# Edge network with one target product per block, numbers to compare in PSUM, and a reordered ScalarE round in attention 1

## The reference

```python
# edge network
edge_in = concatenate([h[src], h[dst], edge_features])
h1 = relu(edge_in @ We1 + be1)            # 32 wide
edge_msg = relu(h1 @ We2 + be2)           # 128 wide
h2 = relu(concatenate([h[dst], edge_msg]) @ Wn1 + bn1)   # 64 wide
out = h + segment_sum(relu(h2 @ Wn2 + bn2), dst)
# attention 1 (4 heads, ELU, softmax with the segment's maximum)
e = elu(s_src[src] + s_tgt[dst]);  ex = exp(e - segment_max(e)[dst])
out = segment_sum(ex / segment_sum(ex)[dst] * xp[src], dst)
# attention 2 (8 heads, leaky Relu, softmax without the maximum)
# relations: each edge's source row times its type's weights, summed into nodes
out = x @ w_self.T;  out[src] += x[dst] @ weights[edge_type]
```

## Time and profile before

| | us |
|---|---|
| median of 3 runs (lowest to highest) | 4735.3 (4725.31 to 4736.79) |
| profiled execution, its own time | 4749.68 |
| span in its profile, first to last instruction | 4747.9 |
| edge network, first gather to last (L1193) | 70.2 to 1164.4 |
| attention 1, the same | 1219.7 to 2354.1 |
| attention 2, the same | 2461.6 to 3516.3 |
| relations, the same | 3657.3 to 4727.2 |

### The profile page before, as it was taken

How to read it: one execution, slowest core, us unless ns; L and a number is a source line. 1 busy time by engine, 2 the same in 40 slices (tenths; PEclk the granted TensorE clock), 3 DMA queues, 4 the chain that set the end, 5 groups by cost and what they waited for, 6 DMA issues and landing times. The chain is left out here.

```text
span 4747.9 us, 82711 instructions
## 1 busy us (share of the span) xinstructions
PE 3500.8 (74%) x18822; PEld 2815.3 (59%) x18822; DVE 2650.5 (56%) x8500; ACT 1355.3 (29%) x4722; POOL 3336.3 (70%) x3373
## 2 busy tenths in 40 slices
PE   4999999999488888888758988889977433334333
PEld 2555555555477777777748877778863333333333
DVE  6677667665356566666665666666555333333332
ACT  4444444443344444444432222222222000000000
POOL 4777777776577777777527777777741777777776
PEclk8999999999555555555565555555558555555555
DMA  4555454441343333433312223332225222222222
GB/s 94 111 105 99 88 88 88 88 91 28 106 99 100 100 101 100 97 100 98 68 39 60 74 72 77 81 86 60 55 72 195 53 51 51 51 51 52 51 51 57
DMA packets 489982, 378.46 MB, mean 80 GB/s; under 512 B 307216, under 2 KB 442170, under 8 KB 486443
## 3 DMA queue, kind: packets, MB, share of 16 engines
q0 software_dynamic: 106496, 184.24, 17.5%
q1 hardware_dynamic: 383272, 192.14, 16.9%
HBM read 327.50 MB, written 33.83 MB: 76 GB/s over the span
## 5 line engine op out<-in xcount | busy, mean ns | idle before, releaser
L1193 POOL DMA_INDIRECT gat_row<-tab,gat_index x832 | 850.0, 1022 | 296.3 <-issue 222.0
L1193 POOL DMA_INDIRECT mlp_row<-tab,mlp_index x832 | 841.6, 1012 | 308.1 <-issue 241.0
L1193 POOL DMA_INDIRECT rel_row<-tab,rel_index x832 | 817.5, 983 | 283.7 <-issue 236.9
L1193 POOL DMA_INDIRECT att_row<-tab,att_index x832 | 802.3, 964 | 265.1 <-issue 250.0
L1564 PE MATMUL rel_ps_sum<-rel_row,rel_hot 128*128 128x128 f32 x1664 | 426.0, 438 | 658.5 <-DMA rel_row<-tab,rel_index 636.3
L1564 PEld LDWEIGHTS rel_ps_sum<-rel_row,rel_hot 128*128 128x128 f32 x1664 | 370.5, 328 | 714.6 <-DVE rel_hot L1587 396.3
L1791 PE MATMUL gat_ps_sum<-gat_row,gat_hot 128*128 128x136 f32 x1664 | 441.6, 446 | 179.4 <-ACT gat_sums L1740 128.9
L1986 PE MATMUL att_ps_sum<-att_row,att_hot 128*128 128x136 f32 x1664 | 443.1, 446 | 121.2 <-DVE acc L1496 116.9
L1791 PEld LDWEIGHTS gat_ps_sum<-gat_row,gat_hot 128*128 128x128 f32 x1664 | 387.6, 330 | 194.4 <-ACT gat_hot L1734 123.1
L1496 DVE TENSOR_TENSOR acc<-acc,rel_ps_sum 128x128 f32 x416 | 119.6, 287 | 678.6 <-PE rel_ps_sum L1564 648.7
L1986 PEld LDWEIGHTS att_ps_sum<-att_row,att_hot 128*128 128x128 f32 x1664 | 379.2, 324 | 196.9 <-DVE acc L1496 192.4
(11 more groups left out here) (275 smaller groups left out, 6092.6 us busy)
## 6 DMA issues: line engine op xcount, KB each, us to landing
mlp_aim<-in_dst SPq DMA_DIRECT2D x416, 128.0 KB
gat_aim<-in_dst SPq DMA_DIRECT2D x416, 128.0 KB
mlp_row<-in_edge_attr SPq DMA_DIRECT2D x416, 64.0 KB
tab<-n_stage SPq DMA_DIRECT2D x25, 1024.0 KB
mlp_row<-tab,mlp_index POOLq DMA_INDIRECT x832
gat_row<-tab,gat_index POOLq DMA_INDIRECT x832
att_row<-tab,att_index POOLq DMA_INDIRECT x832
rel_row<-tab,rel_index POOLq DMA_INDIRECT x832
```

The lines of the kernel that those rows point to most:

```text
L1193: gp.indirect_dma_start(rows[n][b][:, t, :], None, tables[n], bass.IndirectOffsetOnAxis(index[b][:, n, t:t + 1], axis=0)).then_inc(s_g[b], 16)
```

## The change

The target terms of both layers of the edge network become one product of 96 columns (`mm_dst`), written to one of two banks `p_h`, where `h2` has partitions 0 to 63 and `h1` 64 to 95. `h1`, the messages and `h2` are then each one product over all 512 edges of the block, and the last product takes rows 0 to 63 for all four tiles. The halves no longer lie side by side. Sums go to two banks. The numbers 1 to 128 are copied to PSUM at the head of the edge network and of the relations, and `make_hot` compares from there. In attention 1 ACT's round is reordered, and all but `lay` come four rounds later.

```diff
-        h1 = [c.sb(f"h1{b}", [IN_D, HALF]) for b in range(2)]
+        h1 = [c.sb(f"h1{b}", [IN_D, BLOCK]) for b in range(2)]
-        h2 = [c.sb(f"h2{b}", [P, HALF]) for b in range(2)]
+        h2 = [c.sb(f"h2{b}", [HID2, BLOCK]) for b in range(2)]
+        p_row, p_em, p_nm, p_iota = (c.ps(n) for n in "row em nm iota".split())
+        p_h, p_sum = ([c.ps(f"{n}{b}") for b in range(2)] for n in ("h", "sum"))
...
-                act.activation(h1[b % 2][:], p_h1[0:IN_D, 0:HALF], ACT.Relu).then_inc(s_h1r, 1)
+                act.activation(h1[b % 2][HID2:IN_D, :], p_h[b % 2][HID2:IN_D, :], ACT.Relu).then_inc(s_h1r, 1)
...
-                act.activation(h2[b % 2][:], p_h2[:, 0:HALF], ACT.Relu).then_inc(s_h2r, 1)
+                act.activation(h2[b % 2][:], p_h[b % 2][0:HID2, :], ACT.Relu).then_inc(s_h2r, 1)
...
+            def mm_dst(k, q, b):
+                ge(pe, s_h2r, k - 1)
+                pe.wait_ge(s_hot_t, k + 1)
+                pe.wait_ge(s_dst, k + 1)
+                tick(pe, s_tick)
+                for n in range(2):
+                    edges = slice(n * HALF, (n + 1) * HALF)
+                    mm = pe.matmul(p_h[b % 2][0:IN_D, edges], dst[b % RING][:, n, :], hot_t[b % RING][:, edges],
+                                   start=(n == 0), stop=False)
+                mm.then_inc(s_q, 1)
             def mm_h1(k, q, b):
-                for n, edges, to_h1, to_h2 in sides(b):
-                    pe.matmul(to_h1, dst[b % RING][:, n, HID2:IN_D], hot_t[b % RING][:, edges], start=True, stop=False)
-                for n, edges, to_h1, to_h2 in sides(b):
-                    mm = pe.matmul(to_h1, g.we1_row[:], row_t[b % 2][:, edges], start=False, stop=True)
-                mm.then_inc(s_h1, 1)
+                pe.matmul(p_h[b % 2][HID2:IN_D, :], g.we1_row[:], row_t[b % 2][:], start=False, stop=True
+                          ).then_inc(s_h1, 1)
...
-                for n in range(2):
-                    rows = slice(n * HID2, n * HID2 + HID1)
-                    mm = pe.matmul(p_em[:, n, :], g.we2[rows, :], h1[b % 2][rows, :],
-                                   start=True, stop=True)
-                mm.then_inc(s_em, 1)
+                pe.matmul(p_em[:], g.we2[HID2:IN_D, :], h1[b % 2][HID2:IN_D, :], start=True, stop=True).then_inc(s_em, 1)
...
-                for n, edges, to_h1, to_h2 in sides(b):
-                    mm = pe.matmul(to_h2, g.wn1_msg[:], em[b % 2][:, edges], start=False, stop=True)
-                mm.then_inc(s_h2, 1)
+                pe.matmul(p_h[b % 2][0:HID2, :], g.wn1_msg[:], em[b % 2][:], start=False, stop=True).then_inc(s_h2, 1)
...
-                for t in range(2):
-                    for n in range(2):
-                        rows = slice(n * HID2, (n + 1) * HID2)
-                        mm = pe.matmul(p_nm[:, n, t * P:(t + 1) * P], h2[b % 2][rows, t * P:(t + 1) * P],
-                                       g.wn2[rows, :], start=True, stop=True)
+                for t in range(TILES):
+                    mm = pe.matmul(p_nm[:, t * P:(t + 1) * P], h2[b % 2][:, t * P:(t + 1) * P], g.wn2[0:HID2, :],
+                                   start=True, stop=True)
...
-                ge(pe, s_acc, 2 * k)
+                ge(pe, s_acc, 2 * (k - 1))
...
-            pipeline(pe, [(1, turn), (3, mm_h2), (2, mm_h1), (4, mm_sum), (2, mm_em), (3, mm_nm), (2, mm_q)])
+            pipeline(pe, [(1, turn), (3, mm_h2), (2, mm_dst), (2, mm_h1), (4, mm_sum), (2, mm_em), (3, mm_nm)])
...
-            v.memset(p_h1[:], 0.0)
+            ch.do(v.tensor_copy(iota, g.iota[:]))
...
-                v.tensor_tensor(hot[b % RING][:], g.iota[:].unsqueeze(1).broadcast_to([P, TILES, P]),
+                v.tensor_tensor(hot[b % RING][:], iota.unsqueeze(1).broadcast_to([P, TILES, P]),
...
+            v.tensor_copy(iota, g.iota[:]).then_inc(s_iota, 1)
+            v.wait_ge(s_iota, 1)
...
-                v.tensor_tensor(hot[b][:], g.iota[:].unsqueeze(1).broadcast_to([P, TILES, P]),
+                v.tensor_tensor(hot[b][:], iota.unsqueeze(1).broadcast_to([P, TILES, P]),
...
-            pipeline(act, [(0, lay), (0, bring_tgt), (4, at_end(bring_local)), (5, at_end(fifth_exp)),
-                           (6, at_end(to_lanes)), (9, at_end(weight)), (14, measure_gap), (15, make_hot), (19, keep_sum), (21, at_end(fade_exp))], WIDE)
+            pipeline(act, [(0, lay), (4, bring_tgt), (23, keep_sum), (18, measure_gap), (19, make_hot),
+                           (8, at_end(bring_local)), (9, at_end(fifth_exp)), (10, at_end(to_lanes)), (13, at_end(weight)),
+                           (25, at_end(fade_exp))], WIDE)
```

More of the change, by code:

```diff
@@ L1217, in edge_mlp @@
         own = [c.sb(f"own{b}", [P, TILES]) for b in range(2)]
-        p_row, p_h1, p_h2, p_sum = (c.ps(n) for n in "row h1 h2 sum".split())
-        p_em, p_nm = (c.ps(n, (P, 2 * BLOCK))[:].rearrange("p (h f) -> p h f", h=2)[:, :, 0:HALF]
-                      for n in ("em", "nm"))
+        p_row, p_em, p_nm, p_iota = (c.ps(n) for n in "row em nm iota".split())
+        p_h, p_sum = ([c.ps(f"{n}{b}") for b in range(2)] for n in ("h", "sum"))
+        iota = p_iota[:, 0:P]
         s_g, s_tick = c.sems("g", UNROLL), c.sem("tick")
@@ L1316, in em_relu @@
                 ge(act, s_h2, k - 1)
-                act.activation(em[b % 2][:].rearrange("p (h f) -> p h f", h=2), p_em, ACT.Relu,
-                               bias=g.be2[:]).then_inc(s_emr, 1)
+                act.activation(em[b % 2][:], p_em[:], ACT.Relu, bias=g.be2[:]).then_inc(s_emr, 1)
             def h2_relu(k, q, b):
@@ L1401, in mm_sum @@
                 for t in range(TILES):
-                    mm = pe.matmul(half_sum(p_sum, t // HALF_TILES, D + 1), hot[b % RING][:, t, :], nm[b % 2][:, t, :],
+                    mm = pe.matmul(half_sum(p_sum[b % 2], t // HALF_TILES, D + 1), hot[b % RING][:, t, :], nm[b % 2][:, t, :],
                                    start=(t % HALF_TILES == 0), stop=(t % HALF_TILES == HALF_TILES - 1))
                 mm.then_inc(s_sum, 1)
-            pipeline(pe, [(1, turn), (3, mm_h2), (2, mm_h1), (4, mm_sum), (2, mm_em), (3, mm_nm), (2, mm_q)])
+            pipeline(pe, [(1, turn), (3, mm_h2), (2, mm_dst), (2, mm_h1), (4, mm_sum), (2, mm_em), (3, mm_nm)])
         @block.vector
@@ L1458, in nm_relu @@
                 ge(v, s_sum, k - 1)
[L1459 to L1464, removed]
+                v.tensor_tensor(nm[b % 2][:, :, 0:D], p_nm[:].rearrange("p (t f) -> p t f", f=D),
+                                less[:].unsqueeze(1).broadcast_to([P, TILES, D]), ALU.max).then_inc(s_nmr, 1)
+            unrolled([(5, add_sum(nc, v, g, g.bin_d, p_sum, D + 1, 2, s_sum, s_acc, s_tick)), (4, nm_relu),
                       (0, localize), (0, make_hot_t), (0, bring_dst), (2, make_hot)],
@@ L1488, in fn @@
     def fn(k, q, b):
-        bank = p_sum if ring == 1 else p_sum[b % ring]
+        bank = p_sum[b % ring]
         tick(v, s_tick)
@@ L1532, in relation_sum @@
         row = [c.sb(f"row{b}", [P, TILES, D]) for b in range(UNROLL)]
-        p_sum = [c.ps(f"sum{b}") for b in range(2)]
+        p_sum, p_iota = [c.ps(f"sum{b}") for b in range(2)], c.ps("iota")
+        iota = p_iota[:, 0:P]
         s_g, s_word, s_tick = c.sems("g", UNROLL), c.sems("word", UNROLL), c.sem("tick")
-        s_ix, s_hot, s_sum, s_acc, s_node, s_turn, s_loc = (
-            c.sem(n) for n in "ix hot sum acc node turn loc".split())
+        s_ix, s_hot, s_sum, s_acc, s_node, s_turn, s_loc, s_iota = (
+            c.sem(n) for n in "ix hot sum acc node turn loc iota".split())
         block = c.block()
```

5 lines of the change are left out of this document (removed).

## The result

| | before | after |
|---|---|---|
| median of 4 runs each (lowest to highest) | 4734.5 (4725.31 to 4736.79) | 5005.5 (5003.81 to 5012.1) |
| ratio, with its 95% interval | | 1.0579 (1.0561 to 1.0597) |
| profiled execution: own time, span | 4749.68, 4747.9 | 5006.49, 5004.7 |
| predicted: median, profiled execution | | 4992, 5007 |

A forecast was written before the change was run, and what follows sets the result against it. POOL's gathers bound the kernel before; PE would bound the edge network after. Terms +322 - 37 - 28 = +257 on the profiled 4749.7 gave 5007, less 14 for the median: 4992 us, own range 4950 to 5035, stated range 4870 to 5055.

The forecast's parts named there:

- The edge network, +322: Edge network: PE's block grows from 5.09 to 6.81 us, PE becomes the bound; stage 1427 us, before 1105.
- the reading of L1383's 0.58 us: Edge network: four 256-column records, 0.86 us in sequence, fit 0.58 only if side-by-side halves run together: 2 x 0.215 plus 0.15.
- last gather about 320 us later: Edge network: sign expected in the profile after, the stage's last gather coming about 320 us later.
- 11 us for fill and drain: Edge network: added to the stage's time before (1094 to 1105 us) and likewise to the time after.
- The 8 and the 3 us: Edge network after: estimates of 8 us for the start, clock partly at half, and 3 us for waits in the last rounds.
- fixed part: Edge network: time per PE group beyond its streamed columns, taken as 0.10 to 0.21 us depending on weight columns.
- The rival with 0.11: Edge network: message and last product overlap, being in separate rows; 62 to 208 us less, 4784 to 4930; chance 0.11.
- No cover failed: Edge network: ACT's Relu of h1 ends while PE's sum runs; at most 0.3 us per block if that cover fails.
- The releaser: Edge network: sign expected in the profile after, POOL idle with PE's turn as what releases it.
- Attention 1, -37: Attention 1: the new ACT round removes POOL's waits, -31 us, and drain waits, -6 us; bounds -57 to -10.
- the drain, put at 6 us: Attention 1, after the last gather: one or two waits on the sums disappear, saving 6 us.
- The step on `lay`'s four rounds: Attention 1: `lay` four rounds earlier against the rest takes POOL's index waits away too, within the -31 us.

The follow-up runs named there:

- e3: Kernel before with only the new edge network (attention 1's order and relations' comparison as before): 5052.7 us, ratio 1.0675.
- e5b: Kernel after with h2 split again into rows 0-63 and 64-127, last product alternating rows, comparison from SBUF; repeat run: 4919.1 us, 1.0397 to before.
- e6b: Kernel after with the message product over rows 64 to 127, rows 96 to 127 zero; repeat run: 4849.8 us, 1.0249 to before.
- e1: Kernel before with only ACT's new round (order and lags) in attention 1: 4700.8 us, ratio 0.9930.
- e7b: Kernel before with ACT's new order in attention 1 but the old lags; repeat run: 4703.2 us, ratio 0.9939.
- e8b: Kernel before with ACT's old order in attention 1, `lay` four rounds ahead of all the rest; repeat run: 4728.1 us, ratio 0.9999.
- e2: Kernel before with only the relations' numbers 1 to 128 in PSUM for the comparison: 4712.3 us, ratio 0.9955.

## Why the prediction was right, step by step

- **The edge network, +322: measured +321.0 (e3).** Groups predicted from start to start and measured: target terms 1.04 and 1.03, edge rows 0.96 and 0.98, message 1.06 and 1.05, message into h2 1.01 and 1.01, last product 1.08 and 1.08; the block 6.81 and 6.81. The step that carried the forecast was the reading of L1383's 0.58 us as two halves at the same time. e5b shows it: with paired halves the eight records take 0.65, without 1.08.
- **Where the stage's extra time lies.** The sign "last gather about 320 us later" missed: it came 1474.5 - 1164.4 = 310.1 us later. The prediction had kept 11 us for fill and drain on both sides. But from the last gather to the first of attention 1 it is now 1547.5 - 1474.5 = 73.0 us, before 55.3, because PE, now the slower of the two, still has blocks in hand when POOL is through. The 8 and the 3 us had no row, and no run separates them; that the stage's sum was off by only 1 us against e3 is in part luck (the profiles have +323.1 in e3 and +328.2 in the kernel after).
- **One fixed part was passed over.** The prediction gives products with 32 weight columns a fixed part of 0.10 us. L1362 has 32 columns too and takes 0.46 us, only 0.03 above its 0.43. It is followed by L1366, of the same shape; the parts of 0.10 to 0.21 stand where the next group has another shape. In the new round every group is followed by another shape, so the sum did not suffer.
- **No overlap of message and last product.** The rival with 0.11 did not come, and e6b shows why: the two run together as soon as both have the 64-row shape; the separate rows alone did not do it. The Trainium skill (TensorEngine Tiling (Array Packing), Key Properties) has it that a change of tiling mode drains the engine while tiles of one mode run in parallel: 2.13 us and 1.10 us agree. The Trainium skill (TensorE: Matmul & The Clock Gate, Part 3) has it that weight loads overlap running products only when their row groups differ. They differ in the kernel after as in e6b, but in the kernel after the first weights of the last product load at 243.25, with its own start and after the message's 1.05 us; so different row groups are not enough there.
- **No cover failed** in the kernel after: no group of the block shows idle time. Part of the cover was thin, though; e6b takes the last product away as cover and pays 0.33 us per block.
- **The releaser was named wrongly.** POOL's stop was put on PE's turn. It is ACT's indices (445.8 us); the price is the same, since ACT waits for PE.
- **Attention 1, -37: measured -31.0 (e1).** The wait for the copy of the sums is gone and e7b and e8b show that the order did it. POOL's idle time before its gathers fell from 296.3 to 266.5. The term that was too large is the drain, put at 6 us: first gather to last gained 29.1 us and first gather to the next stage 30.5, which leaves 1.4 for it. The step on `lay`'s four rounds failed too: that lag alone is worth nothing measurable (0.9999), and of the waits on indices, 32.3 us before, 20.5 are left. VectorE's held-up gathers did not shift: busy time 850.0 before and 851.8 after.
- **Relations, -28: measured -19.4 (e2).** The mechanism holds, the size was read from one profiled execution, in which more gathers than usual were held up: 108 over 1 us, against 49 to 88 in the four others. It lies just outside the bounds of this term, -31 to -20.
- **The sum.** Between the profiled executions 5004.7 - 4747.9 = +256.8, the +257 of the forecast; between the medians +271. The forecast took over the 14 us by which the profile of before stood above its median, and the profile of after stands 1 above its own. The gathers of every later run on a chip at normal speed are shorter (944 ns against 947, some 10 us over 3328), and the relations' excess was above its mean: together enough for those 14 us, which belonged to that one execution and not to profiling as such. That 5007 was hit to a microsecond is therefore luck: the 14 us that the forecast took over were not there, and 14 us of its terms were missing. Against the medians, two terms were 6 and 9 us too favourable and the edge network's 1 too dear: 14 us, the distance from 4992 to 5005.5.

## What to carry to other kernels

Where PE is level with the bound, count its time in columns streamed one after the other: merging two products into one saves an instruction, but if the old ones lay side by side in the array and ran together, as here, the merged one streams twice as many columns behind each other. Here products ran together only in tiles of one shape, so padding a narrow one with zero rows can bring back what separate rows alone do not; then look at once for the wait whose cover was the time just saved. In an engine's round put first what another engine waits for, before what only its own next group needs.

## What the runs showed of the hardware

- Two products of different tile shape, 32 and 64 rows, in separate rows of the array, take 2.13 us, and 1.10 us when the narrower is padded to 64 rows.
- A gather that starts inside the comparison with two tensors in SBUF ends 0.81 to 0.84 us after the comparison does, but for a few at its very edges; one that starts 0.10 us before it, or inside it with one tensor in PSUM, takes its 0.94 us. Over 832 gathers, moving one comparison's operand to PSUM took the longest gather from 1459 to 961 ns. The Trainium skill (GPSIMD Engine Reference, Key points) names work with two SBUF inputs as one that contends with GpSimd, and the trace agrees.
- How many gathers are held up depends on how the two engines happen to fall: the same unchanged stage lasted 1051.5 to 1070.0 us in five executions, with 49 to 108 gathers of over 1 us.
- The same chip ran all kernels, the one before too, in 5848.0 us at one time and in 4730.4 later. PE's groups lasted the same (the last product of e5 took 249.48 - 248.84 = 0.64 us then and 0.65 later). What slowed the transfers stays open.
